# A convolution and a split-precision feed-forward block: convolution outputs staged over DRAM, weights turned where they are loaded, first steps in another order

## The reference

```python
out = conv1d(x, weight, padding=4, groups=4)            # 9 taps, 32 channels in 4 groups of 8
out = out + (cond @ c_weight.T)[:, :, None] + bias[None, :, None]
xt  = out.reshape(4096, 512)
y   = (silu(xt @ W_gate.T) * (xt @ W_up.T)) @ W_down.T  # W_gate, W_up: 1376 x 512; W_down: 512 x 1376
result = x + y.reshape(128, 32, 512)
```

## Time and profile before

| | us |
|---|---|
| median of three runs | 772.33 |
| the profiled execution | 771.86 |
| its span | 770.1 |
| TensorE busy (97% of the span) | 749.5 |
| VectorE busy (56%) | 433.3 |
| ScalarE busy (36%) | 275.9 |
| GpSimd busy (14%) | 104.5 |

### The profile page before, as it was taken

The page is one execution under the profiler, slowest core; times in us unless marked ns, Lnnn a source line. Parts: engine busy times, 40 slices in busy tenths (PEclk is TensorE's granted clock), DMA queues, the critical chain, the costliest instruction groups (busy, mean ns, idle before and its releaser), DMA issues.

```text
span 770.1 us, 10317 instructions
## 1 busy us (share of the span) xinstructions
PE 749.5 (97%) x3459; PEld 610.6 (79%) x3459; DVE 433.3 (56%) x702; ACT 275.9 (36%) x518; POOL 104.5 (14%) x133
## 2 busy tenths in 40 slices
PE   7669999999999999999999999999999999999998
PEld 6548888878888888887888888887788888887886
DVE  4797676774485554555844555455663444445224
ACT  3365555453442323324431333323442233333221
POOL 5446646320000101000100100100000000000000
PEclk9989999999999999999999999999999999999999
DMA  5566866478997676676543967767444776776402
GB/s 169 131 221 220 264 216 231 169 238 267 376 307 252 202 209 188 188 203 189 186 134 114 313 184 200 209 201 206 151 136 123 271 207 192 192 193 177 149 27 110
DMA packets 113687, 152.38 MB, mean 198 GB/s; under 512 B 11139, under 2 KB 49187, under 8 KB 113635
## 3 DMA queue, kind: packets, MB, share of 16 engines
q1 hardware_dynamic: 111904, 150.93, 63.4%
q10 hardware_dynamic: 1730, 0.79, 0.4%
HBM read 108.95 MB, written 34.34 MB: 186 GB/s over the span
## 4 chain that ended last, share of the span: by engine, by line
PE 95%; DVE 2%; ACTq 1%; issue 1%; ACT 0%; DMA 0%; SPq 0%; DVEq 0%
PE bank L676 55%; PE bank L708 31%; PE bank L589 2%; PE bank L594 2%; PE bank L571 2%; ACTq L888 1%; DVE hc_lo L972 1%; PE bank L632 1%; PE bank L603 1%; PE bank L614 0%; DVE g_all L1163 0%; ACT hc_hi L767 0%; PE bank L552 0%; DVE ring L972 0%; DVE g_all L1060 0%
## 5 line engine op out<-in xcount | busy, mean ns | idle before, releaser
L676 PE MATMUL bank<-hc_hi,ring 128*128 128x512 f32 (+1 forms) x1232 | 386.8, 395 | 10.7 <-DVE hc_lo L972 7.3
L676 PEld LDWEIGHTS bank<-hc_hi,ring 128*128 128x128 f32 (+1 forms) x1232 | 225.1, 186 | 62.2 <-issue 9.4
L676 PE MATMUL bank<-hc_lo,ring 128*128 128x512 f32 (+1 forms) x616 | 241.1, 391 | 0.0
L708 PE MATMUL bank<-ring,g_hi 128*128 128x512 f32 (+1 forms) x704 | 218.5, 392 | 0.0
L767 ACT ACTIVATE mix<-bank 128x512 f32<-128x512 f32 (+1 forms) x132 | 78.8, 597 | 209.7 <-PE bank L676 209.7
L708 PEld LDWEIGHTS bank<-ring,g_hi 128*128 128x128 f32 (+1 forms) x704 | 131.2, 188 | 27.9 <-DVE g_lo L972 0.8
L708 PE MATMUL bank<-ring,g_lo 128*128 128x512 f32 (+1 forms) x352 | 137.1, 390 | 0.0
L676 PEld LDWEIGHTS bank<-hc_lo,ring 128*128 128x128 f32 (+1 forms) x616 | 114.4, 186 | 26.9
L972 DVE TENSOR_TENSOR g_lo<-g_all,g_hi 128x512 fp32r<-128x512 f32 (+1 forms) x88 | 60.9, 694 | 83.8 <-ACT g_hi L767 83.8
L767 ACT ACTIVATE g_hi<-g_all 128x512 fp32r<-128x512 f32 (+1 forms) x88 | 55.1, 629 | 114.0 <-PE bank L708 114.0
L1129 DVE TENSOR_TENSOR mix<-bank,mix 128x512 f32<-128x512 f32 (+1 forms) x44 | 30.4, 691 | 93.5 <-ACT mix L870 93.5
(11 more groups left out here) (126 smaller groups left out, 548.9 us busy)
## 6 DMA issues: line engine op xcount, KB each, us to landing
ring<-saved SPq DMA_DIRECT2D x319, 256.0 KB, 3.0
saved<-ring SPq DMA_DIRECT2D x99, 256.0 KB, 2.6
g_all<-in_x SPq DMA_DIRECT2D x32, 256.0 KB, 3.6
out_y<-g_all SPq DMA_DIRECT2D x32, 256.0 KB, 3.4
x_in<-in_x SPq DMA_DIRECT2D x13, 512.0 KB, 5.2
stage<-win SPq DMA_DIRECT2D x96, 64.0 KB, 2.4
w_nat<-in_L_ffn_W_gate SPq DMA_DIRECT2D x10, 256.0 KB, 3.0
w_nat<-in_L_ffn_W_up SPq DMA_DIRECT2D x10, 256.0 KB, 3.5
```

Of the source, the lines that this page charges most:

```text
L676: mm = pe.matmul(bank[0:w, :], wt, hv, start=fresh and q == 0 and t == 0, stop=q == 1 and t == 2, skip_group_check=not fresh)
L708: mm = pe.matmul(acc(half, tt)[:], gs, wd, start=f == 0 and t == 0, stop=f == FC - 1 and t == 2)
```

## The change

1. Staging goes over a DRAM tensor `turned`. `spill` writes the windows of a chunk (in group 0 two DMAs of 256 KB, one for each convolution step; else one of 512 KB) in pieces of 512 bytes; `fetch` waits until the spills have landed and reads the chunk back in natural order with two DMAs of 256 KB in rows of 2 KB. All of them are on SyncE; ScalarE's staging DMAs are gone. In groups 1 to 3 a fetch stands one loop step behind its spill.
2. As positions are now in natural order, `permute` becomes `wrap` (only the small copy of 4 columns stays), and the transposes read `w_nat`. Weight loads wait for the transposes instead of the permuting copies.
3. The loads of the context weights go to ScalarE's queue; the filter's transpose waits for its own load alone. The context products of group 0 come first, those of groups 1 to 3 behind the first convolution step. TensorE does a convolution step before the transposes that stood ahead of it. The low parts of the first filter matrices are made from PSUM.
4. ScalarE and VectorE split and mix in another order: all reads of the convolution first, then what needs chunks 0 and 1, then chunk 2 and `prepare(1, 0)`, then chunk 3.

The core of the diff:

```diff
+        turned = nc.dram_tensor("turned", [KC, JJ, R, CG, P], F32, kind="Internal").ap()
...
+        def spills(grp, i):
+
+            return 2 * (i + 1) if grp == 0 else KC * (grp + 1) + i + 1
...
-                        sp.wait_ge(permuted[kind], f - NNAT // 2 + 1)
+                        sp.wait_ge((gate_turned, up_turned)[kind], f - NNAT // 2 + 1)
...
-            def stage_chunk(grp, i, channels=range(CG)):
-                sp.wait_ge(conv_out, CPG * grp + 2 * i + 3)
-                for o in channels:
-                    sp.dma_start(stage[:, o // OB, i, (o % OB) * P:(o % OB + 1) * P],
-                                 windows(grp, i)[o:P:CG, :, :]).then_inc(staged[o // OB][i], LD)
+            def spill(grp, i, k0=0, k1=2):
+
+                sp.wait_ge(conv_out, CPG * grp + 2 * i + k1 + 1)
+                w0, w1 = k0 * WB, k1 * WB
+                sp.dma_start(turned[i, w0:w1].rearrange("w r o n -> (r o) w n"), windows(grp, i)[:, w0:w1, :]).then_inc(spilled, LD)
+
+            def fetch(grp, i):
+                sp.wait_ge(spilled, LD * spills(grp, i))
+                for half in range(2):
+                    sp.dma_start(stage[:, half, i, :], turned[i].rearrange("w r o n -> (w r) (o n)")[:, half * TOK:(half + 1) * TOK]
+                                 ).then_inc(staged[half][i], LD)
...
             sp.dma_start(conv_w_nat, conv_w.rearrange("o c k -> o (c k)")).then_inc(small_in, LD)
-            sp.dma_start(ctx_w_nat, ctx_w).then_inc(small_in, LD)
-            sp.dma_start(cond_nat, cond).then_inc(small_in, LD)
             load_x(0, 0)
             load_x(0, 1)
             load_nat(0)
             load_x(0, 2)
             load_x(0, 3)
             load_nat(1)
-            stage_chunk(0, 0)
-            stage_chunk(0, 1, range(OB))
-            stage_chunk(0, 2, range(OB))
-            load_nat(2)
-            stage_chunk(0, 3, range(OB))
+            for i in range(KC):
+                spill(0, i, 0, 1)
+                spill(0, i, 1, 2)
+                fetch(0, i)
+                if i == 1:
+                    load_nat(2)
             sp.wait_ge(x_blocked, 1)
...
             save_products(0)
-            load_nat(3)
...
                 for f in range(FC):
+                    if g == 0 and f + 3 < FC:
+                        load_nat(f + 3)
...
                     if g == 0 and f + 1 < FC:
                         save_products(f + 1)
-                    if g == 0 and f + 4 < FC:
-                        load_nat(f + 4)
...
+                    if g + 1 < G and 3 <= f <= 9 and f % 2 == 1:
+                        fetch(g + 1, (f - 3) // 2)
                     if g + 1 < G and f % 2 == 0 and 2 <= f <= 8:
-                        stage_chunk(g + 1, f // 2 - 1)
+                        spill(g + 1, f // 2 - 1)
...
-            def permute(f):
+            def wrap(f):
...
                 for kind in range(2):
                     slot = (2 * f + kind) % NNAT
                     pool.wait_ge(nat_loaded[slot], LD * ((2 * f + kind) // NNAT + 1))
                     pool.tensor_copy(w_nat[0:w, slot, L:ROW], w_nat[0:w, slot, 0:PAD]).then_inc(nat_wrapped, 1)
-                    pool.wait_ge(nat_wrapped, 2 * f + kind + 1)
-                    if f > 0:
-                        pool.wait_ge((gate_turned, up_turned)[kind], f)
-                    pool.tensor_copy(perm[0:w, kind, :].rearrange("f (i p j) -> f i p j", i=KC, p=R),
-                                     w_nat[0:w, slot, PAD:ROW].rearrange("f (i j p) -> f i p j", i=KC, p=R)
-                                     ).then_inc(permuted[kind], 1)
...
-                pe.wait_ge(small_in, 3 * LD)
-                pe.transpose(xt_ps[0:CG * TAPS, 0:CH], conv_w_nat, ident[0:CH, 0:CH])
+                pe.wait_ge(small_in, LD)
+                pe.transpose(xt_ps[0:CG * TAPS, 0:CH], conv_w_nat, ident[0:CH, 0:CH]).then_inc(setup_t, 1)
+                pe.wait_ge(ctx_in, 2 * LD)
                 pe.transpose(up_ps[:, 0:CH], ctx_w_nat, ident[0:CH, 0:CH])
-                pe.transpose(gate_ps[:, 0:P], cond_nat, ident[:]).then_inc(setup_t, 1)
...
-                pe.wait_ge(permuted[0], f + 1)
+                pe.wait_ge(nat_wrapped, 2 * f + 1)
                 if f > 0:
                     pe.wait_ge(gate_kept, f)
                 for i in range(KC):
-                    mm = pe.transpose(gate_ps[:, i * P:i * P + w], perm[0:w, 0, i * P:(i + 1) * P], ident[0:w, 0:w])
+                    mm = pe.transpose(gate_ps[:, i * P:i * P + w], w_nat[0:w, 2 * f % NNAT, PAD + i * P:PAD + (i + 1) * P], ident[0:w, 0:w])
...
             toep_products()
             turn_x(0, 0)
             turn_x(0, 1)
-            ctx_products()
+            ctx_products((0,))
+            conv_head(0)
             turn_x(0, 2)
-            conv_head(0)
             for k in range(STEPS):
+                conv_step(0, k)
                 if k + 3 < STEPS:
                     turn_x(0, k + 3)
+                if k == 0:
+                    ctx_products(range(1, G))
                 if k == 2:
                     turn_gate(0)
                 if k == 3:
                     turn_up(0)
-                conv_step(0, k)
...
-            def stage_second(i):
-                act.wait_ge(conv_out, 2 * i + 3)
-                for o in range(OB, CG):
-                    act.dma_start(stage[:, 1, i, (o - OB) * P:(o - OB + 1) * P], win_first[o:P:CG, i, :, :]).then_inc(staged[1][i], LD)
-
+            act.dma_start(ctx_w_nat, ctx_w).then_inc(ctx_in, LD)
+            act.dma_start(cond_nat, cond).then_inc(ctx_in, LD)
             act.dma_start(bias_row, bias.rearrange("(a o) -> a o", a=1)).then_inc(bias_loaded, LD)
...
+            def keep_ctx(n, groups):
+                act.wait_ge(ctx_mm, n + 1)
+                hi(ctxb[:, groups, :], up_ps[:].rearrange("p (g n) -> p g n", g=G)[:, groups, :]).then_inc(ctx_done, 1)
+
+            keep_ctx(1, slice(0, 1))
...
+                if k == 1:
+                    keep_ctx(2, slice(1, G))
                 if 2 <= k <= 5:
                     prepare(0, k - 2)
-                if k in (4, 6):
-                    stage_second(k // 2 - 1)
-                if k >= 6:
-                    split_h(0, RAW_A1, k - 6)
-            stage_second(3)
...
             copy_chain(0, 0, 0)
+            prepare(1, 0)
             for kind in (RAW_A2, K_S1, K_S2):
                 split_h(0, kind, 1)
-            prepare(1, 0)
...
+                t = [part[:].rearrange("p (q o) -> p q o", o=CG) for part in (ta_lo, ta_hi, tb_lo, tb_hi)]
+                if grp == 0:
+                    q0 = QN // 2
+                    in_bank = [part[:, 0:q0 * CH].rearrange("p (q g o) -> p g q o", g=G, o=CG)[:, grp, :, :] for part in (setup_a, setup_b)]
+                    lo(t[0][:, 0:q0 - HALO, :], in_bank[0][:, HALO:q0, :], t[1][:, 0:q0 - HALO, :])
+                    lo(t[0][:, q0 - HALO:, :], in_bank[1][:, :, :], t[1][:, q0 - HALO:, :])
+                    lo(t[2][:, R - HALO:, :], in_bank[0][:, 0:HALO, :], t[3][:, R - HALO:, :]).then_inc(t_lo_done, 1)
...
-                    for half in range(2):
-                        if i > 0:
-                            dve.wait_ge(staged[half][i - 1], LD * OB * (grp + 1))
-                        else:
-                            dve.wait_ge(staged[half][KC - 1], LD * OB * grp)
+                    dve.wait_ge(spilled, LD * (spills(grp, i) - 1))
...
             for k in range(STEPS):
                 if k + 2 < STEPS:
                     split_x(0, k + 2)
+                read_conv(0, k)
                 if 2 <= k <= 4:
                     prepare(0, k - 2)
-                read_conv(0, k)
-                if k >= 6:
-                    split_h(0, RAW_A1, k - 6)
+            for kind in (RAW_A1, K_S3):
+                split_h(0, kind, 0)
+                split_h(0, kind, 1)
...
+            prepare(1, 0)
             mix_h_first(K_S1, 1)
             mix_h_first(K_S2, 1)
-            split_h(0, K_S1, 1)
-            split_h(0, K_S2, 1)
-            prepare(1, 0)
+            for kind in (RAW_A2, K_S1, K_S2):
+                split_h(0, kind, 1)
```

More of the change, by code:

```diff
@@ L183, in adaln_ffn @@
         nat_wrapped = sem("nat_wrapped")
-        permuted = [sem("gate_permuted"), sem("up_permuted")]
         x_blocked_first = sem("x_blocked_first")
@@ L207, in adaln_ffn @@
         conv_out = sem("conv_out")
+        spilled = sem("spilled")
         staged = [[sem(f"staged{half}_{i}") for i in range(KC)] for half in range(2)]
@@ L495, in mix_h_first @@
                 for half in range(2):
-                    pool.wait_ge(staged[half][q], LD * OB)
+                    pool.wait_ge(staged[half][q], LD)
                 pool.tensor_tensor(s_first[K_S3][:, q, :], stage[:, 0, q, :], stage[:, 1, q, :], ALU.subtract).then_inc(s_done[K_S3], 1)
@@ L539, in ctx_products @@
                 pe.wait_ge(consts, 8)
-                for g in range(G):
+                if groups[0] > 0:
+                    pe.wait_ge(ctx_done, 1)
+                for g in groups:
```

(12 more changed lines are left out.)

56 lines of the change are left out of this document (25 added, 31 removed).

## The result

| | before | after |
|---|---|---|
| median of 20 runs, us | 774.50 | 771.74 |
| lowest to highest | 772.03 to 776.68 | 769.16 to 773.42 |
| profiled execution, us | 771.86 | 769.16 |
| its span, us | 770.1 | 767.4 |

The ratio is 0.9965, with a 95% interval of 0.9954 to 0.9976: faster by 0.35%. The profiled execution of the kernel after is the fastest of its twenty. The forecast of the profiled execution was 768.4 (measured 769.16). The forecast of the median was 768.8 (measured 771.74), while the median of the kernel before, 772.33 in three runs, is 774.50 in twenty. The forecast gain was 3.5 us; the medians differ by 2.76. 771.74 lies within the range given, 766.0 to 773.0.

The account below looks back on a forecast made before the run. TensorE was taken as the bound, with time to win only before 57 us. Product (0, 5) moves from 56.10 to 52.6, gaining 3.5: span 766.6, plus 1.76 gives 768.4, plus 0.47 gives 768.8 us; range 766.0 to 773.0.

Parts of the forecast that it names:

- the last term of the sum: From profiled execution to median: the median of the runs, 772.33, lies 0.47 us above it, so 768.4 becomes 768.8.
- Bound and milestone: TensorE bounds the kernel; product f = 0, kind 5 starts at 52.6 instead of 56.10, with 714.0 us behind it unchanged.
- The clock at the start: TensorE runs at half rate until 16.4 us, so 0.9 us brought forward is worth about 0.6 at full rate.
- Start: First loads and transposes of x: 0.9 us earlier; low parts of the filter matrices take 0.27 us alone, counted 0.
- Convolution: VectorE's reads of the convolution: read 5 at 28.4 and read 7 at 30.8, the last over 4 us earlier.
- Relay: Spill, wait and fetch on SyncE: spill 3.1 us, fetch 3.2; chunk 3 lands at 40.35, 0.6 us later than before.
- VectorE's backlog: Sum S1 of the last quarter at 41.3, then 13.75 - 1.57 (prepare moved) - 0.9 (GpSimd copies gone) = 11.3 us to the milestone.
- A: Rival, staging: quick relay with spills at 2.0 and fetches at 2.3 us, milestone 49.8, time 766.0; chance 0.13.
- C: Rival, staging: dear relay, spills 4.6 and fetches 3.8, chunk 3 at 45.45; 773.0 alone, 775.5 with TensorE's pause; chance 0.08.
- D: Rival: ScalarE's in-order queue still binds the milestone, gain not passed on beyond about 2 us; 770.4, chance 0.12.
- B: Rival: after TensorE's longer pause the clock stays at 1.2 GHz 3.4 us longer; milestone 54.8, time 771.0; chance 0.18.

Follow-up runs that it names:

- x9: The kernel before, unchanged, run again for its profile: one execution of 774.62 us.
- x14: The kernel before, unchanged, run once more for its profile: one execution of 775.03 us.
- x13: The kernel after, unchanged, run again for its profile: one execution of 773.37 us.
- x15: The kernel after, unchanged, run once more for its profile: one execution of 773.32 us.
- x12: The kernel after with spills of chunks 2 and 3 ahead of chunk 2's fetch, and context products of groups 1 to 3 behind product 0: 768.77 us, ratio 0.9921.
- x11: The kernel after with prepare(1, 0) put back behind the splits of chunk 3 on ScalarE and VectorE: 772.66 us, ratio 0.9979 to before.
- x10: The kernel after, unchanged, run for its profile: one execution of 771.34 us.
- x4: The kernel after with 29 never-read matmuls added ahead of the two halves of product 1: 773.44 us, ratio 0.9986 to before.

## Where the prediction was wrong, and where it was right

The step that failed is the last term of the sum, "the median of the runs is 772.33, 0.47 above it". By twenty runs of each kernel the median lies 774.50 - 771.86 = 2.64 us above the profiled execution before, and 771.74 - 769.16 = 2.58 above it after. Of the 2.9 us by which the median was missed, 2.1 are this term and 0.8 the execution itself (769.16 against 768.4).

- **That term.** Three runs gave 0.47. Of the twenty runs of the kernel before 7 lie at 772.03 to 772.93 and 13 at 774.31 or above, none between; the three known ahead held two of the lower ones, and the profiled execution, with an early rise of the clock, is of that kind (x9 and x14, with a late one, took 2.8 and 3.2 us more). After has 5 of 20 at 769.16 to 769.95 and 15 at 771.37 or above, and three of its four profiles are 2.2 to 4.2 us above the first. So the forecast was laid onto the faster group. Group by group the medians differ by as much as the whole: 772.30 and 769.55 in the lower, 774.89 and 772.06 in the upper, 2.8 us in both. The milestones of single profiles (1.9 us apart in the late ones, 3.2 or 1.8 in the early) scatter about that with the relay: x13 and x15 are slower than 19 of the twenty runs.
- **Bound and milestone: right.** All the gain lies ahead of 57 us, and span less milestone was 713.9 to 715.2 in every execution above. Of the 3.20 us at the milestone 0.5 is given back behind it, within that spread.
- **The clock at the start: misread.** "Until 16.4 us TensorE runs at half rate" rests on the one row of 16 to 17 us. In that trace TensorE ran at full rate from 9.6 to 13.0 and at half from 13.0 to 16.4: the two context matmuls in a row took 0.48 there and 0.79 in x9. The second fall came at 40.3, not 40.7.

```profile
11.34 0.48 PE L543 MATMUL bank<-g_all 1*128 1x128 f32 x2
```

- **Start: half of what was forecast.** The transposes of x start at 6.90 instead of 7.39, 0.5 us earlier and not 0.9. The low parts took 0.35 us. The new order did more: read 1 was done at 17.24 (forecast 18.9), read 3 at 22.42 (24.0), read 5 at 27.96 (28.4).
- **Convolution: right at its end.** Read 7 ends at 31.24 (30.47 + 0.77); forecast 30.8.
- **Relay: right within 0.7 us where it matters.** Fetches of chunks 2 and 3 were issued at 31.74 and 36.65; forecast 32.4 and 36.75. Those of chunks 0 and 1 came at 19.59 and 24.76, over 2 us ahead of the forecast 22.0 and 27.1; 0.8 of that is the spills, which landed 2.3 us after the last issue, against 3.8 and 3.5 for chunks 2 and 3. From 15 to 45 us a spill took 3.4 us and a fetch 3.0 in the median; forecast 3.1 and 3.2. By the Trainium skill's page "DMA: Bandwidth & Descriptors" (section "Why small descriptors are slow (HBM only)") the spill was an estimated 3.3. The median of the trace lies nearer to that than to 3.1, but single spills of the same pieces lie from 2.3 us up, so nothing here shows that the piece size is the cause.
- **VectorE's backlog: the mechanism right, one term wrong and two left out.** S1 came at 40.79, forecast 41.3. The way from there was forecast as 13.75 - 1.57 - 0.9 = 11.3 and measured 12.11. The wrong step is the 0.9 "while GpSimd permuted weights, copies that are gone": the permuting copies went, but the x_blk copy, which stood beside the sum S2 before (it took 1.40 us), runs beside the two splits now, and they take 2.18 us as ever. In x12, where that copy falls on S2 again, the pair takes 1.28. Before (VectorE, then GpSimd), then after:

```profile
43.14 1.40 DVE L1079 TENSOR_TENSOR g_all<-g_all,stage 128x512 f32<-128x512 f32 x1
42.45 1.53 POOL L274 COPY x_blk<-x_in 128x512 f32<-128x512 f32 x1 [10.65 <-DMA x_in<-in_x]
44.64 1.44 POOL L473 COPY perm<-w_nat 128x512 f32<-128x512 f32 x1
```

```profile
41.59 0.69 DVE L1088 TENSOR_TENSOR g_all<-g_all,stage 128x512 f32<-128x512 f32 x1
42.20 0.68 DVE L980 TENSOR_TENSOR hc_lo<-stage,hc_hi 128x512 fp32r<-128x512 f32 x1
```

  And x12:

```profile
43.95 1.28 DVE L988 TENSOR_TENSOR hc_lo<-g_all,hc_hi 128x512 fp32r<-128x512 f32 x2
```

  The way lost 13.75 - 12.11 = 1.64 us: 1.57 for prepare, as forecast (0.7 for its work, x11, and the rest for the copy that ran beside it), 0.7 for S2, which the forecast did not count, less 0.6 for a split of `stage` that stood ahead of S1 and now stands behind it, which it did not count either (the three agree with 1.64 within 0.1). With 0.5 won ahead and 0.8 missed behind, 52.6 became 52.90.
- **Rivals.** A's quick relay came for the spills of chunks 0 and 1 alone, and C's dear one not at all in the first profile (fetches at 3.0, spills at 3.4). C's own sum has a slip: with spills at 4.6 the fetches of chunk 0 hold SyncE until 24.3, so chunk 3 lands at 46.2 and not 45.45, and the time is 773.7 and not 773.0. D fell: the wait for "issue" went from 3.4 to 0.6. B's longer low clock came in x10, x13 and x15, to between 50.3 and 52.1 us, but not its price: from S1 on x13 and x15 take the same 12.11 us, and x10 0.24 more. What made them slower besides the late rise is the relay, by 1.2 to 1.8 us.

What stays open: what decides the moment of the rise, since work from 1.46 us on did not move it; what makes the relay 0.8 to 2.2 us longer in some executions, and whether x4's matmuls had a part in it.

## What to carry to other kernels

Before a forecast is laid onto a profiled execution, ask which group of the runs it belongs to: where a median rests on three runs and the clock's rise differs by execution, 2 to 3 us of 770 hang on it. A path over several landings of DMA has a spread of its own (up to 2.2 us here), and one profile shows one draw of it. When an engine's contention is to vanish with a neighbour's work, look at what the neighbour does next, for it may move into the same place. And a pause that can't be closed is a place for work that stands in the way elsewhere: moving 2.4 us of small products into it gave 0.3% more, by the medians, on top of the earlier spills, almost as much as the whole change, though the intervals of the two overlap at their ends.

## What was not expected of the hardware

By the durations of its matmuls TensorE first reached full rate at 8.8 to 9.6 us in some executions and at 14.0 to 21.2 in others of the same or nearly the same program. A VectorE instruction of 128x512 that takes 0.64 us in a pair took about 1.1 beside a GpSimd copy of the same shape. And a spill pair issued at the same microsecond (32.6) landed by 36.65 in one execution and by 38.45 in another.
